# Four transformer layers on one core: the loops over the passes of a layer written out

## What is computed

```python
x = _L0_xattn_ref(x, ctx_1024, ...)
x = _L1_xattn_ref(x, ctx_1024, ...)
x = _L2_xattn_ref(x, ctx_1024, ...)
x = _L3_xattn_ref(x, ctx_1024, ...)
return x
```

## Time and profile before

| | us |
|---|---|
| median of 3 runs | 2274.79 (2274.24 to 2275.49) |
| the profiled execution | 2274.92 |
| its span, first to last instruction | 2273.2 |
| TensorE matmuls busy | 1921.8 (85%) |
| TensorE weight loads busy | 1507.4 (66%) |
| VectorE busy | 1307.1 (57%) |
| GpSimd busy | 996.9 (44%) |
| ScalarE busy | 967.8 (43%) |
| DMA, mean | 15 GB/s |

### The profile page before, as it was taken

The page is one execution under the profiler, slowest core; times in us unless marked ns, Lnnn a source line. Parts: engine busy times, 40 slices in busy tenths (PEclk is TensorE's granted clock), DMA queues, the critical chain, the costliest instruction groups (busy, mean ns, idle before and its releaser), DMA issues.

```text
span 2273.2 us, 32499 instructions
## 1 busy us (share of the span) xinstructions
PE 1921.8 (85%) x10497; PEld 1507.4 (66%) x10497; DVE 1307.1 (57%) x2218; ACT 967.8 (43%) x2274; POOL 996.9 (44%) x1235
## 2 busy tenths in 40 slices
PE   4666667677887887887999899998988999999997
PEld 3565556454664655664777677777766787787776
DVE  5877778658558558658444465454533635436361
ACT  1111221224334333334546465564644665556563
POOL 5566665535335336345333454434533423333330
PEclk8889998677877887887999999999988999999999
DMA  7100000000200000000000200000000000000000
GB/s 216 69 5 5 9 5 5 5 1 6 79 1 5 5 0 5 5 0 5 6 1 6 79 0 9 0 5 5 1 5 5 6 6 0 5 23 0 9 1 10
DMA packets 31292, 34.88 MB, mean 15 GB/s; under 512 B 3196, under 2 KB 30040, under 8 KB 30808
## 3 DMA queue, kind: packets, MB, share of 16 engines
q1 hardware_dynamic: 31192, 33.70, 4.8%
HBM read 31.60 MB, written 2.10 MB: 15 GB/s over the span
## 4 chain that ended last, share of the span: by engine, by line
PE 60%; DVE 11%; issue 4%; POOL 2%; ACT 2%; DVEq 0%; POOLq 0%; ACTq 0%
PE ps L503 31%; PE ps L670 9%; PE ps L701 8%; PE ps L680 6%; PE ps L514 3%; DVE xn L874 2%; DVE rowmax L1010 1%; DVE rowsum L1016 1%; PE ps L696 1%; PE ps L668 1%; DVE work L1012 1%; DVE work L1004 1%; DVE O L845 1%; POOL x_all L1126 1%; DVE stats L864 0%
## 5 line engine op out<-in xcount | busy, mean ns | idle before, releaser
L503 PE MATMUL ps<-hT,w_slot 128*128 128x256 f32 x1856 | 455.1, 399 | 21.1 <-ACT hT L744 21.1
L503 PEld LDWEIGHTS ps<-hT,w_slot 128*128 128x128 f32 x1856 | 359.7, 199 | 77.8 <-ACT hT L744 24.0
L1190 POOL TENSOR_TENSOR work<-KT,own_head 128x512 f32<-128x512 f32 x256 | 261.5, 1047 | 288.6 <-ACT KT L756 234.3
L680 PEld LDWEIGHTS ps<-ident,work 128*128 128x128 f32 x1536 | 206.4, 154 | 178.3 <-issue 110.6
L670 PE MATMUL ps<-work,QT 128*128 128x512 f32 x512 | 276.5, 622 | 22.8 <-POOL work L1190 20.6
L680 PE MATMUL ps<-ident,work 128*128 128x128 f32 x1536 | 265.5, 301 | 35.6 <-POOL work L1199 35.6
L1199 POOL TENSOR_SCALAR work<-work,winv 128x128 f32<-128x128 f32 x512 | 184.9, 384 | 218.9 <-DVE winv L1029 218.4
L886 DVE TENSOR_TENSOR x_all<-ps,x_all 128x512 f32 (+1 forms) x88 | 60.7, 690 | 379.6 <-PE ps L503 326.9
L829 ACT ACTIVATE work<-work,rowmax 128x128 f32<-128x128 f32 x768 | 245.0, 392 | 68.1 <-DVE rowmax L1008 66.5
L701 PEld LDWEIGHTS ps<-V,work 128*128 128x128 f32 x2048 | 251.2, 192 | 7.4 <-issue 4.4
L701 PE MATMUL ps<-V,work 128*128 128x17 f32 x2048 | 248.9, 254 | 2.4 <-ACT work L818 2.4
(11 more groups left out here) (119 smaller groups left out, 3015.6 us busy)
## 6 DMA issues: line engine op xcount, KB each, us to landing
ctx_in<-in_ctx SPq DMA_DIRECT2D x32, 256.0 KB, 2.7
w_slot<-in_L_xattn_W SPq DMA_DIRECT2D x2, 1024.0 KB, 6.4
w_slot<-in_L_xattn_ff_w SPq DMA_DIRECT2D x1, 2048.0 KB, 11.2
w_slot<-in_L_xattn_ffn_w SPq DMA_DIRECT2D x2, 1024.0 KB, 9.9
w_slot<-in_L_xattn_w SPq DMA_DIRECT2D x2, 1024.0 KB, 9.3
out<-x_all SPq DMA_DIRECT2D x8, 256.0 KB, 2.1
x_all<-in_x SPq DMA_DIRECT2D x1, 1536.0 KB, 11.7
pad<-in_mask_Bx1x1xS_fk SPq DMA_DIRECT2D x1, 1024.0 KB, 6.7
```

Of the source, the lines that this page charges most:

```text
L503: mm = pe.matmul(dst, lhsT(k), rhs(k), start=(k == 0), stop=(k == chunks - 1))
L680: mm = pe.transpose(bank(2 + u % 2)[:, tok(h)], prob[u % NP][:, tok(h)], ident[:, :])
L1190: pool.tensor_tensor(KB[u % NK].rearrange("p (h k) -> p h k", h=HU), keys, own_head[:, half * HU:(half + 1) * HU].unsqueeze(2).broadcast_t ...
```

## The change

Every loop over passes is unrolled by the program that writes the kernel: `for g in range(...)` in place of a loop of the engine, in `passes` (all four computing engines) and twice on SyncE. g is then a number everywhere, so each wait has a constant and each address is fixed; the tests `isinstance(g, int) and g == 0`, which told the straight lines from the loop, become tests of g alone. The order of the work, the tiles, the buffers and the number of passes are as before. The instruction streams grow: three copies of a pass stand where one stood.

```diff
@@ passes
             for layer in range(NL):
-                with eng.Fori(0, NG - 1) as g:
+                for g in range(NG - 1):
                     one_pass(layer, g, (layer, g + 1))
                 before_last(layer)
                 one_pass(layer, NG - 1, (layer + 1, 0) if layer + 1 < NL else None)
@@ x_of; the same in load_ctx, the stores, stage, sum, post, bias, keep and pad
-            return x_all[:, bass.ds(seq(g, st, j), 1), :]
+            return x_all[:, seq(g, st, j):seq(g, st, j) + 1, :]
@@ SyncE
-                with sp.Fori(1, NG - 1) as g:
+                for g in range(1, NG - 1):
                     load_ctx(g + layer * NG, g)
@@ SyncE, stores
-            with sp.Fori(0, NG) as g:
+            for g in range(NG):
                 for st in range(ST):
@@ TensorE, ScalarE: the same test at four other places
-                        if isinstance(g, int) and g == 0:
+                        if g == 0:
@@ TensorE, ot
-                        if st == 1 and layer == NL - 1 and isinstance(g, int) and n["out"] == PER_PASS["out"][layer] - 1:
+                        if st == 1 and layer == NL - 1 and g == NG - 1 and n["out"] == PER_PASS["out"][layer] - 1:
@@ TensorE, first piece of the feed-forward
-                            if layer < NL - 1 or not isinstance(g, int):
+                            if layer < NL - 1 or g < NG - 1:
                                 pe.wait_ge(q["ctx_ready"], use("ctx", layer, g, 0) + 2)
@@ ScalarE, stage
-                            if not isinstance(g, int) or g > 0:
+                            if g > 0:
                                 act.wait_ge(s["x_rest"], 16)
@@ GpSimd, spread
-                    if u == 0 and layer == 1 and mix == 0 and st == 0 and isinstance(g, int):
+                    if u == 0 and layer == 1 and mix == 0 and st == 0 and g == 0:
                         pool.wait_ge(s["o_ready"], G * phase("mix", layer, g, mix, st))
```

More of the change, by code:

```diff
@@ L421, in load_ctx @@
                     sp.wait_ge(c[st]["ctx_ps"], t)
-                    sp.dma_start(ctx_in[st][:, :, :], ctx_view[:, bass.ds(seq(g, st), G), :]).then_inc(c[st]["ctx_loaded"], 16)
+                    sp.dma_start(ctx_in[st][:, :, :], ctx_view[:, seq(g, st):seq(g, st) + G, :]).then_inc(c[st]["ctx_loaded"], 16)
             sp.dma_start(x_all[:, 0:first, :], x_view[:, 0:first, :]).then_inc(s["x_first"], 16)
@@ L453, in _ @@
                     load_ctx((layer + 1) * NG, 0)
-            with sp.Fori(0, NG) as g:
+            for g in range(NG):
                 for st in range(ST):
                     sp.wait_ge(c[st]["yadd_done"], G * use("yadd", NL - 1, g, PER_PASS["yadd"][NL - 1]))
-                    sp.dma_start(out_view[:, bass.ds(seq(g, st), G), :], x_all[:, bass.ds(seq(g, st), G), :]).then_inc(s["stored"], 16)
+                    sp.dma_start(out_view[:, seq(g, st):seq(g, st) + G, :], x_all[:, seq(g, st):seq(g, st) + G, :]).then_inc(s["stored"], 16)
             sp.wait_ge(s["stored"], 16 * NG * ST)
@@ L561, in emit @@
                                 .then_inc(q["qk_ps"], 1)
-                        if isinstance(g, int) and g == 0 and st == 0:
+                        if g == 0 and st == 0:
                             pe.wait_ge(s["vrows_loaded"], 16 * len(COLUMNS))
@@ L630, in step @@
                     def step(i):
-                        if i == 0 and st == 0 and isinstance(g, int) and g == 0:
+                        if i == 0 and st == 0 and g == 0:
                             pe.wait_ge(s["tables_ready"], 1)
@@ L738, in emit @@
                         act.wait_ge(q["tin_ps"], use("tin", layer, g, 0))
-                        act.activation(xc[st], x_all[:, bass.ds(seq(g, st), G), :], ACT.Copy).then_inc(q["xc_ready"], 1)
+                        act.activation(xc[st], x_all[:, seq(g, st):seq(g, st) + G, :], ACT.Copy).then_inc(q["xc_ready"], 1)
                     elif piece == "tin":
@@ L763, in emit @@
                             act.wait_ge(q["qk_ps"], G * use("local", layer, g, 0) + j + 1)
-                            act.activation(KT[st][:, j, :], b[:, D:2 * D], ACT.Copy, scale=keep[:, bass.ds(seq(g, st, j), 1)])\
+                            act.activation(KT[st][:, j, :], b[:, D:2 * D], ACT.Copy, scale=keep[:, seq(g, st, j):seq(g, st, j) + 1])\
                                 .then_inc(q["locK_ready"], 1)
@@ L884, in emit @@
                             dve.wait_ge(q["xc_ready"], use("stage", layer, g, n["stage"]))
-                        xs = x_all[:, bass.ds(seq(g, st), G), :]
+                        xs = x_all[:, seq(g, st):seq(g, st) + G, :]
                         dve.tensor_tensor(xs, b.rearrange("p (g d) -> p g d", g=G), xs, ALU.add).then_inc(q["yadd_done"], G)
@@ L1000, in shift @@
                         if arg["mask"] == "pad":
-                            m = pad[:, bass.ds(seq(g, st, j), 1), :].broadcast_to([P, HU, S])
+                            m = pad[:, seq(g, st, j):seq(g, st, j) + 1, :].broadcast_to([P, HU, S])
                         else:
```

## The result

The straight kernel takes 2251.13 us in the median of four runs (2250.13 to 2253.52), the kernel before 2274.51 (2272.61 to 2275.49): a ratio of 0.990, 95% interval 0.988 to 0.992. That is 23.4 us, where I forecast 8.9 and a range that ended at 2260. The profiled execution took 2250.39 us.

The account below looks back on a forecast made before the run. Hand-overs between engines bound it, with TensorE's matmuls most of the chain and no engine saturated. Layers 0 to 3 and tail: 0 - 6.5 - 2.1 - 1.6 - 0.1 = -10.3, plus 1.4 for clock, -8.9: 2266 us, range 2260 to 2271.5.

Parts of the forecast that it names:

- The holes: VectorE's idle stretches after layer 1's two branches back, 2.75 and 2.79 us, would go: -5.5 us as lower bound.
- rival 2: Instruction supply: straight lines fetch nearly 40 more code pages in layers 1 to 3, +10 us, 2285; chance 0.04.
- The sum of layer 1 at an unchanged clock: Layer 1's three looped passes together gain 6.5 us, bounds -5.5 and -7.8.
- the 3.4 for p1: Layer 1's second looped pass gains 3.4 us, counting half its 1.76 us excess over the third as bad luck.
- The clock: TensorE's clock: one additional drop at a pass entry in layer 2, costing +1.4 us.
- Register work: Arithmetic for pass-dependent waits, mostly hidden on busy engines; 0.09 us read at layer 3's masked addition, few in line.
- The yardstick: Layer 1's third looped pass against its already straight last pass at GpSimd's bias addition: 2.6 us gain from straight code.
- p0 of layer 1: Layer 1's first looped pass, with no hole in front, gains between 0.16 and 0.65 us, taken as 0.5.
- Layer 3: Its three looped passes gain 1.6 us, bounds -0.3 and -3, with the exponential's table load moved onto the path.
- 1 (the clock takes the gain back): Layer 2's looped passes all start at low clock and layer 1's run unluckily: -3.3 us, 2271.5; chance 0.14.
- 3 (only the holes): Only idle stretches behind branches in layers 1 and 3 count, register arithmetic being covered: -4.7 us, 2270; chance 0.14.
- 4 (more comes back): Upper bounds of layers 1 and 2 with no additional clock drop: -13.4 us, 2261.4; chance 0.10.

Follow-up runs that it names:

- The early load: Straight kernel plus a tiny exponential after the last Gelu of each feed-forward step in layers 1 and 3: 2246.3 us, again 2246.6 against 2251.5 straight.
- the two shifted ones: Kernel before, loops kept, with some 0.9 or about 2 us of small VectorE reductions ahead of its first energy product: 2272.7 and 2269.7 us.

## Why the prediction was wrong, and where it was right

**The holes: right.** I took 5.5 us for layer 1's two; put back at 7.3 they cost 7.9. No hole came at the 42 additional code pages of TensorE (I said nearly 40), so rival 2 is refuted.

**The sum of layer 1 at an unchanged clock, -6.5: right by TensorE's idle time,** which is 6.4 us lower in the mean of six straight kernels against four looped ones. That it fits so well is in part luck: the 3.4 for p1 held 0.9 of clock (half of the 1.76 between p1 and p2), and the registers' share was too small. Over all layers TensorE's idle time fell by 7.8 us where the sum said 10.3.

**The clock: the step that failed.** The prediction took +1.4, one additional low entry into layer 2, and let every rival about the clock lose time. That entry came: p2 of layer 2 starts at the lower level and takes 146.36 us, above the 143.1 that I named as a sign of error, and the layer as a whole gained nothing, -0.7 forecast and +0.3 measured. What I left out are layers 0 and 1, whose passes ran at a mean clock of 0.78 to 0.85 before and had time to give back. It came to -12.0 us in layer 1 and -5.3 in layer 0, where I had written 0 with bounds of 1. In layer 0 the second product with V is still preceded by 6.84 us of idle, as forecast, and TensorE's idle time even rose by 1.7. The gain there is the clock's: p3, unchanged code, took 129.9 to 130.0 us in all six kernels in which VectorE's layer 0 was a loop, and 126.7 to 127.8 in all others; what in the loop does this was not tried.

**Register work: the term that was mis-sized.** "Few of these are in line" and "where the engine is busy the queue runs ahead" gave it 0.16 us in a pass of layer 1 and at most 0.65 for p0. Put back alone in layer 1, the registers cost 9 us in the whole kernel and 12.5 in layer 1's one profile, 9.1 of it in p0 to p2. Their idle part is small (3.0 us). The rest is matmuls run at the lower level. I had read the price from layer 3's masked addition, 0.09 us. At the start of layer 1 the delays are larger and come one behind the other: 0.18 us at V's rounding, 0.48 by TensorE's next wait for VectorE, and 0.15 in 5.3 us of VectorE's work. The kernel before would have told: there TensorE starts 0.23 us behind V's rounding in p0 and 0.05 in p3.

**The yardstick.** I read the surviving gain at GpSimd's addition, 2.6 us, as p2 against p3. Measured, p2 gained 4.25 there. p3's 85.13 was itself the clock's: the same code needs 83.67 now. One execution of p3 is no measure finer than 1.5 us in a layer whose clock wavers.

**p0 of layer 1:** forecast -0.5, got -5.5 in the profile (170.7 to 165.2) and about -2.5 in the mean (165.2 to 169.9 in nine straight kernels, 167.1 to 170.9 in five looped ones). The two ranges overlap, so the single -5.5 is not to be trusted. It has no hole, so what it gains is the registers' and the clock's; with registers put back it took 170.2.

**Layer 3: right, -1.6 forecast and -1.2 measured.** L1117 comes 63.4 us after the start in p1 and p2, 63.5 forecast:

```profile
1923.90 0.22 POOL L1117 TENSOR_SCALAR vareps<-meanvar 128x2 f32<-128x2 f32 x1 [5.51 <-DVE meanvar L867]
...
2057.14 0.22 POOL L1117 TENSOR_SCALAR vareps<-meanvar 128x2 f32<-128x2 f32 x1 [5.51 <-DVE meanvar L867]
```

The masked addition follows 0.35 us of idle in p2 as well:

```profile
2062.02 0.69 DVE L1004 TENSOR_TENSOR work<-ps,drop 128x512 f32<-128x512 f32 x1 [0.35 <-PE ps L670]
```

And the table load moved onto the path, as forecast: where layer 3 was looped but ScalarE's hole was absent (with only layer 1 straight), p1 and p2 took 132.80 us, less than the 133.23 of straight code. The early load took that back and more: the exponential's table is loaded twice in a pass, and in the loop only one of the two stood off the path. With both moved a pass is 1.57 us shorter than in straight code.

**The rivals.** 1 (the clock takes the gain back) had the right engine and the wrong sign. 3 (only the holes) is refuted by the registers put back. 4 (more comes back) was nearest, 2261.4, but for want of a clock term it stopped 10 us short. The range's low end, 2260, was rival 4 rounded down: it held the bounds of the code and none for the clock in its favour.

**Open.** Why 3 us of idle time, spread in pieces of 0.1 to 0.3, bring the lower level for so much longer was not taken apart: the registers were put back at one moment only, part of their cost fell where no code was edited (p3, layer 2), and no run shows by what step the clock follows them. Nor was it tried what ScalarE's and GpSimd's registers cost alone, or those of layer 0, or what both engines' registers cost at another moment.

## What to carry to other kernels

Where TensorE's clock falls in a stretch, cost an edit there twice: once as idle time, and once as the clock, with a range to both sides; here the second was twice the first in the one profile and one and a half times in layer 1's means. Look for the price of register arithmetic where one engine starts on another's result, and compare the same hand-over in the loop and in its straight last pass; the queue's instructions on the chain are not in themselves a delay, as long as the engine works through them. When an edit is put back alone, compare the parts it did not touch as well. And a loop's body hides where the compiler places table loads; when it is written out, place them by hand.

## What the runs showed of the hardware that I had not expected

**The hint moves the stall to the exit.** Announcing the branch back took VectorE's idle time before the first reduce of p1 and p2 from 2.75 and 2.71 us to 0.24 and 0.20, and cost stops of 1.03 us on TensorE and 2.69 on GpSimd once, where the loop of layer 1 ended. With three trips that is no gain.

**The same loop body stalls in one kernel and not in another.** ScalarE's 1.72 us in layer 3 were absent when only layer 1 was straight: the load stood at 1868.58 with no idle before it, from the same loop. In the four kernels whose ScalarE code is that of the kernel before (itself, the two shifted ones, and the one with only VectorE straight) they are there, 1.72 to 2.04 us. That the place of the code decides fits this, and was not tested by itself.

**GpSimd nearly doubles its time beside VectorE.** In the looped kernel shifted by 2.5 us VectorE got to its first sum of layer 0's output 1.2 us sooner (37.81 against 39.03), although it had 2.5 us more to do. Energy products of GpSimd before the first pass, in the kernel before and then in the shifted one:

```profile
14.59 7.28 POOL L1155 TENSOR_TENSOR work<-QT,KT 128x1024 f32<-128x1024 f32 x2 [9.10 <-ACT QT L767]
24.15 5.71 POOL L1155 TENSOR_TENSOR work<-QT,KT 128x1024 f32<-128x1024 f32 x2 [2.28 <-PE ps L627]
```

```profile
14.86 3.81 POOL L1160 TENSOR_TENSOR work<-QT,KT 128x1024 f32<-128x1024 f32 x2 [9.38 <-ACT QT L767]
22.84 3.81 POOL L1160 TENSOR_TENSOR work<-QT,KT 128x1024 f32<-128x1024 f32 x2 [4.17 <-PE ps L627]
```

Two products take 7.28 us where VectorE runs its own product of two operands (15.98 to 20.08) beside them, and 3.81 where VectorE's begins only at 19.23, behind the small reductions. The Trainium skill, GPSIMD Engine Reference, section Specifications, says that GpSimd shares its way to SBUF with VectorE and contends with VectorE's instructions that have two SBUF inputs; these rows agree. At the start of layer 1 the shifted kernel is 2.7 us ahead (479.87 against 482.56), and its median was 3.4 us below that of the kernel before in the same rounds. The 6.7 us that layer 0 lost when all engines but VectorE were straight fit this too: eight products of VectorE took 0.82 us more each.
